# The first layer's output projection, norms and quantised FFN as one stage by query block; the pair attention's output products dealt over two steps

## The chip, the cores and the metric

The program runs on one core of a Trainium2 chip. The metric is the device time of one execution in microseconds, median of three runs. A profiled execution has a time of its own, and a span (first to last instruction) a little shorter.

## The reference

Four layers over the same residual stream of 8 sequences of 256 tokens, 128 wide (2048 tokens in all; here 16 tiles of 128 tokens, 4 query blocks of 512). Each layer is a gated cross-attention followed by a gated FFN, both on a layer norm of the stream:

```python
x = x + tanh(g_xattn[n]) * cross_attention_n(layernorm(x), ctx)
x = x + tanh(g_ffn[n])   * ffn_n(layernorm(x))
```

The change touches layer 0, and the attention of layers 1 and 3. Layer 0's attention has 16 heads of width 8. Its result goes through an output projection of 128x128. Its FFN is fake-quantised: both activations are rounded to integers against the largest absolute value over the *whole* tensor, so that nothing of the first product can start before all 2048 normalised tokens are known, and nothing of the second before all of the hidden tensor is known.

```python
def _act_fake_quant(x, clip_factor):
    scale = sigmoid(clip_factor) * max(abs(x)) / 127
    return clip(round(x / scale), -128, 127) * scale
xq = _act_fake_quant(x, clip_x)                       # 2048 x 128
h  = silu(xq @ quant(w_gate).T) * (xq @ quant(w_up).T)   # 2048 x 352
y  = _act_fake_quant(h, clip_down) @ quant(w_down).T
```

Layers 1 and 3 have 16 heads of width 64, attended over 256 keys within a sequence, with an output projection of 1024x128.

## The kernel before, in words

The program is a chain of stages. Each stage is an `nc.Block()`: five instruction streams (TensorE "pe", ScalarE "act", VectorE "dve", GpSimd "pool", SyncE "sp") that run in the order in which they are written and wait for each other on semaphores; all engines meet at the end of a block. After most blocks `retire` clears that stage's semaphores, one instruction each, on GpSimd, before GpSimd may go on to the next block. PSUM has 8 banks of 512 columns, `ps[:, bank, :]`.

**Layer 0 between its attention and layer 1** is five blocks, each over all 2048 tokens:
1. `attention_small_heads` ends: the last heads are stored to DRAM (`o_dram`), and SyncE waits for these stores (L567).
2. `gathered_projection` (L1511): the heads come back from DRAM, tile by tile, as 128x128 (L1521, 16 DMAs on two queues), are transposed (L1533), copied (L1547), multiplied by `wo0` (L1538) and added to the stream `M.x` (L1554).
3. `layernorm` (L414): statistics (L438 to L450) in two halves of 8 tiles, `rstd` by a power on GpSimd (L468), 16 normalisations (L455), 16 transposes (L475), and four copies (L486).
4. `quantised_ffn` (L1559): the largest value along each partition (L1607), then over the partitions by GpSimd's `partition_all_reduce` (L1600); three passes over 2048 columns that scale, round and clip (L1619 to L1621); 12 jobs (query block, chunk of the 352 hidden columns), each a gate product, an up product, a SiLU on ScalarE (L1594) and a multiply on VectorE (L1626). Then the largest hidden value: three reductions of 2048 columns (L1631), a second all-reduce (L1602), nine passes of rounding (L1641 to L1644), 48 fp32 down products (L1666), and four additions to the stream (L1649).
5. `layernorm` again, for layer 1 (with hi/lo fp16 copies, L488, L461). Then `attention_pairs` begins; its engines wait for two memsets of GpSimd (L846, L847) before the first product (L909).

**`attention_pairs`** (L787, layers 1 and 3) works on *units*: a query block and a pair of heads, 32 in each layer; a unit is two *half* steps `i` (one sequence each). The order is written out by hand: in step `i` TensorE issues

```python
scores(i + 1)         # L876 x12, then waits for r_done(i + 1), then L884 x8
max_scores(i + 2)     # L897
queries_keys(i + 3)   # L909 to L914
turn(i // 2 - 1)      # even steps, L960: 4 fp32 transposes
values((i + 1) // 2)  # odd steps, L924 to L926: 12 products
project((i - 3) // 2) # odd steps, L972 to L976: 12 products
weighted(i)           # L948 to L952: 24 products; max_rows(i + 2), L931, in their middle
```

VectorE issues in the same step: `normalised(i-1)` (L1056, L1058), `largest(i+2)` (L1065, after L897), `queries_keys` (L1079, after ScalarE's L1018), `turned` (even, L1086) or `values` (odd, L1093), `add` (odd, once in 8 units, L1101) and `max_rows(i+2)` (L1073), which gives r_done(i+2). ScalarE: the exponentials (L1005, after L884), L1018, L1024 or L1030, L1012. GpSimd: two subtractions L859 for each half.

## Time and profile before

| | us |
|---|---|
| median of 3 runs | 2148.47 (2147.4 to 2151.1) |
| the profiled execution | 2147.12 |
| its span | 2145.3 |
| layer 0, last head to layer 1's first product (L770 to L909) | 106.25 |
| TensorE / VectorE / ScalarE / GpSimd busy over the span | 82% / 62% / 59% / 52% |

The page gives the busy share of each engine over the whole span and in 40 slices; with the stages so different, a window for each stage says more. TensorE's busy time is modelled: overlapping products are counted from issue to end, so that the starts of neighbouring rows show better than the busy share where it waits. "Idle before" in a row is the time that the engine stood still before it, and what ended it.

### The profile page before, as it was taken

What the parts mean: (1) busy time and instruction counts of PE and PEld (TensorE: products, weight loads), DVE (VectorE), ACT (ScalarE), POOL (GpSimd) and SP (SyncE); (2) the same over time, 40 slices, a digit from 0 to 9 for tenths busy, and PEclk for the clock granted to TensorE, in tenths of its full rate; (3) what the DMA queues carried; (4) which work ended last, traced back from release to release, by engine and by line L of the source; (5) the groups of instructions that cost most, each with busy time, mean ns of one, the idle gap of its engine ahead of it and who ended that gap; (6) DMA issues with size and microseconds to landing.
All of it is one profiled execution on the core that took longest, in us unless ns stands there. A gap on an engine that the chain in (4) does not pass through costs nothing. (4 is left out here: it accounts for less than half of the span.)

```text
span 2145.3 us, 55182 instructions
## 1 busy us (share of the span) xinstructions
PE 1769.2 (82%) x22168; PEld 1236.0 (58%) x22169; DVE 1329.7 (62%) x2556; ACT 1272.8 (59%) x1627; POOL 1109.8 (52%) x1052
## 2 busy tenths in 40 slices
PE   1699636999947769999999999999736839999778
PEld 1244325888845626666666666666535727888645
DVE  3767376888864366555555555555244547888765
ACT  3357423777734326777777777777624527777553
POOL 2100003555542337777777777777752336775534
PEclk9779858999968859999999999999957969999899
DMA  6401100000032010000000000000122111000000
GB/s 175 80 6 11 27 0 2 3 3 3 2 102 74 25 47 11 11 14 11 10 13 12 11 10 14 11 10 11 32 83 56 36 48 34 3 3 3 2 6 16
DMA packets 95263, 55.20 MB, mean 26 GB/s; under 512 B 43341, under 2 KB 88728, under 8 KB 94918
## 3 DMA queue, kind: packets, MB, share of 16 engines
q1 hardware_dynamic: 86820, 42.61, 8.2%
q0 software_dynamic: 3584, 6.36, 0.9%
q8 instruction: 181, 2.97, 0.6%
q10 hardware_dynamic: 4610, 2.71, 0.5%
q14 instruction: 68, 0.56, 0.1%
HBM read 30.16 MB, written 13.75 MB: 20 GB/s over the span
## 5 line engine op out<-in xcount | busy, mean ns | idle before, releaser
L1422 POOL TENSOR_TENSOR aw_p_lo<-aw_p,aw_p_hi 128x512 f16<-128x512 f32 x512 | 576.5, 1158 | 191.0 <-issue 168.8
L1438 DVE TENSOR_REDUCE aw_max_part<-ps 128x1 f32<-128x512 f32 x512 | 351.2, 690 | 289.7 <-PE ps L1244 284.9
L859 POOL TENSOR_TENSOR ap_p_lo<-ap_p,ap_p_hi 128x512 f16<-128x512 f32 x256 | 291.0, 1158 | 181.6 <-issue 173.9
L1374 ACT ACTIVATE aw_p<-ps 128x1024 f32<-128x1024 f32 x256 | 260.0, 1015 | 206.1 <-PE ps L1275 204.0
L1289 PE MATMUL ps<-ctx_hi_lo,aw_p_hi 128*128 128x97 f16 x2048 | 288.9, 206 | 2.5 <-POOL aw_p_lo L1422 2.5
L1291 PE MATMUL ps<-ctx_hi_lo,aw_p_hi 128*128 128x96 f16 x2048 | 288.0, 207 | 0.0
L1293 PE MATMUL ps<-ctx_hi_lo,aw_p_lo 128*128 128x97 f16 x2048 | 287.4, 204 | 0.0
L1381 ACT ACTIVATE aw_p_hi<-aw_p 128x1024 f16<-128x1024 f32 x256 | 270.6, 1057 | 8.1
L1291 PEld LDWEIGHTS ps<-ctx_hi_lo,aw_p_hi 128*128 128x128 f16 x2048 | 197.9, 97 | 25.2
L1289 PEld LDWEIGHTS ps<-ctx_hi_lo,aw_p_hi 128*128 128x128 f16 x2048 | 196.5, 96 | 12.1 <-POOL aw_p_lo L1422 4.7
L1293 PEld LDWEIGHTS ps<-ctx_hi_lo,aw_p_lo 128*128 128x128 f16 x2048 | 201.9, 99 | 0.0
L1244 PE MATMUL ps<-ctxT_hi,aw_queries 96*128 96x512 f16 x512 | 197.4, 390 | 4.6 <-DVE aw_max_part L1438 4.5
L1265 PE MATMUL ps<-aw_queries,aw_keys 128*128 128x512 f16 x512 | 195.7, 382 | 0.8 <-ACT aw_p L1374 0.7
L1266 PE MATMUL ps<-aw_queries,aw_keys 128*128 128x512 f16 x512 | 195.3, 381 | 0.0
L1005 ACT ACTIVATE ap_p<-ps 128x1024 f32<-128x1024 f32 x128 | 131.1, 1024 | 95.0 <-PE ps L884 95.0
L1065 DVE TENSOR_REDUCE ap_neg_max<-ps 128x4 f16<-128x1024 f32 x128 | 156.8, 1225 | 45.6 <-PE ps L897 45.6
L468 POOL TENSOR_TENSOR ln_rstd<-ln_var_eps,neg_half 128x8 f32<-128x8 f32 x10 | 16.5, 1658 | 302.7 <-DVE ln_var_eps L450 238.5
L2178 POOL DMA_INDIRECT result_scratch<-sf_y,sf_token_at x64 | 63.7, 995 | 158.9 <-ACT sf_y L2368 144.2
L1012 ACT ACTIVATE ap_p_hi<-ap_p 128x1024 f16<-128x1024 f32 x128 | 134.8, 1053 | 0.0
L948 PE MATMUL ps<-ap_v_hi,ap_p_hi 128*128 128x65 f16 x1024 | 113.3, 194 | 4.6 <-POOL ap_p_lo L859 4.3
L950 PE MATMUL ps<-ap_v_lo,ap_p_hi 128*128 128x64 f16 x1024 | 113.2, 192 | 0.0
L952 PE MATMUL ps<-ap_v_hi,ap_p_lo 128*128 128x65 f16 x1024 | 112.6, 193 | 0.0
(464 smaller groups left out, 4979.8 us busy)
## 6 DMA issues: line engine op xcount, KB each, us to landing
sf_weights_raw<-in_L_w SPq DMA_DIRECT2D x24, 256.0 KB, 4.2
slot_scratch<-at_empty_rows SPq DMA_DIRECT2D x16, 260.0 KB
sf_fetched<-slot_scratch SPq DMA_DIRECT2D x16, 260.0 KB, 2.9
sf_weights_raw<-in_L_w SPq DMA_DIRECT2D x8, 512.0 KB, 3.9
x_norm<-result_scratch SPq DMA_DIRECT2D x8, 256.0 KB, 4.0
aw_queries<-aw_queries SPq DMA_DIRECT2D x32, 64.0 KB, 1.9
aw_queries<-aw_q_lo SPq DMA_DIRECT2D x32, 64.0 KB, 2.0
raw<-in_L_q SPq DMA_DIRECT2D x3, 512.0 KB, 11.9
```

Source lines behind the costliest of these rows:

```text
L859: nc.gpsimd.tensor_tensor(p_lo[:, i % 2, h, :], p[:, i % 2, h, :], p_hi[:, i % 2, h, :], ALU.subtract).then_inc(lo_done, 1)
L1065: nc.vector.tensor_reduce(NM[:, i % 2, :].rearrange("p (h r) -> p h r", h=2)[:, :, 0:2], ps[:, MB:MB + 2, :].rearrange("p h (t k) -> p h t ...
L1244: nc.tensor.matmul(ps[:, max_bank(b, k), :], S1[0:DC, b % 4, t * P:(t + 1) * P], M.ct_hi[0:DC, kb * QB:(kb + 1) * QB], start=True, stop=Tr ...
L1265: nc.tensor.matmul(o, K1[:, ks], S1[:, c, :], start=True, stop=False)
L1266: nc.tensor.matmul(o, K2[:, ks], S2[:, c, :], start=False, stop=False)
L1289: nc.tensor.matmul(o, p_hi[:, n % 4, cols], M.cv[:, kt, 0:DA], start=kt + t == 0, stop=False, skip_group_check=True)
L1291: nc.tensor.matmul(o[:, 0:DC], p_hi[:, n % 4, cols], M.cv[:, kt, VW:VW + DC], start=False, stop=False, skip_group_check=True)
L1293: ins = nc.tensor.matmul(o, p_lo[:, n % 4, cols], M.cv[:, kt, 0:DA], start=False, stop=kt == NT - 1, skip_group_check=True)
L1374: nc.scalar.activation(p[:, n % 2, :].rearrange("p (b q) -> p b q", b=2), s, ACT.Exp, scale=1.0 / QS).then_inc(exp_done, 1)
L1381: nc.scalar.activation(p_hi[:, n % 4, :], p[:, n % 2, :], ACT.Copy).then_inc(hi_done, 1)
L1422: nc.gpsimd.tensor_tensor(p_lo[:, n % 4, cols], p[:, n % 2, cols], p_hi[:, n % 4, cols], ALU.subtract).then_inc(lo_done, 1)
L1438: nc.vector.tensor_reduce(mpart[:, b % 2, k:k + 1], ps[:, max_bank(b, k), :], AX.X, ALU.max).then_inc(m_done, 1)
```

## The change

`gathered_projection`, `quantised_ffn`, and the two `layernorm` calls around them (layer 0's second and layer 1's first) are replaced by one block, `first_ffn`, that works by query block q (4 tiles):

- The gather of blocks 0 to 2 is issued by SyncE inside the attention (before block 2 of the next query block's heads); the last one right after the stores, two DMAs on each of two queues.
- Projection, addition, statistics, power (of 128x4 instead of 128x8) and normalisation run by block; the largest values are taken from `M.xn`, before the transposes.
- The maximum over the partitions is no longer an all-reduce on GpSimd. VectorE makes a diagonal matrix of the column, TensorE multiplies it by ones (fp32), and VectorE reduces the PSUM row.
- The rounding has two passes (min, then max and + ROUND) of 512 columns; the subtraction of ROUND, with the conversion to bf16 or fp16, goes to ScalarE (VectorE for the first block).
- The hidden maxima are taken job by job, between the multiplies.
- The down product takes fp16 integers and a down weight split into two fp16 halves: 96 fp16 products instead of 48 fp32 ones. The weights' split is made in `prepare`, by six instructions instead of three.
- The addition, layer 1's statistics, norm, transposes and hi/lo copies follow in the same block.
- `retire` has 36 semaphores to clear behind the new block.

In `attention_pairs` the 12 products of `project` are dealt: 6 in the odd step, as before, and 6 in the next even step. `add` goes to the even step, and the loop runs one step longer.

```diff
@@ build
-            layernorm(nc, M, 2 * n, split=True, plain=False)
+            if n != 1:
+                layernorm(nc, M, 2 * n, split=True, plain=False)
             if n == 0:
-                attention_small_heads(nc, M)
-                gathered_projection(nc, M)
+                gathered = [nc.alloc_semaphore(f"gathered{q}") for q in range(NQ)]
+                attention_small_heads(nc, M, gathered)
+                first_ffn(nc, M, gathered)
+                continue
...
-            layernorm(nc, M, 2 * n + 1, split=False, plain=True)
-            quantised_ffn(nc, M)
@@ prepare
-                    nc.vector.tensor_copy(M.wdT[0:IC[c], c, :], M.ps[0:IC[c], 2, c * P:(c + 1) * P])
+                    o = M.ps[0:IC[c], 2, c * P:(c + 1) * P]
+                    link(nc.vector.tensor_scalar(M.wd_hi[0:IC[c], c, :], o, WDS, None, ALU.mult))
+                    nc.vector.scalar_tensor_tensor(M.wd_lo[0:IC[c], c, :], o, WDS, M.wd_hi[0:IC[c], c, :],
+                                                   ALU.mult, ALU.subtract)
@@ attention_small_heads, sync
+                def gather(q):
+                    for i in range(2):
+                        sp.wait_ge(o_stored[i], 2 * (q + 1) * 4 * 16)
+                    for t in range(q * TQ, (q + 1) * TQ):
+                        gather_tile(sp, t)
                 for b in range(NB):
                     qb, g = block_of(b)
+                    if g == 2 and qb:
+                        gather(qb - 1)
@@ attention_pairs
-        steps = range(-3, NH + 2)
+        steps = range(-3, NH + 3)
...
-                    for t in range(TQ):
+                    for t in (2 * half, 2 * half + 1):
...
-                    if i % 2 and is_unit((i - 3) // 2):
-                        project((i - 3) // 2)
+                    if is_unit((i - 3) // 2):
+                        project((i - 3) // 2, 1 - i % 2)
...
-                    if i % 2 and is_unit((i - 3) // 2) and (i - 3) // 2 % NP == NP - 1:
-                        add((i - 3) // 2 // NP)
+                    if i % 2 == 0 and is_unit(i // 2 - 2) and (i // 2 - 2) % NP == NP - 1:
+                        add((i // 2 - 2) // NP)
@@ first_ffn, tensor
+                for q in range(NQ - 1):
+                    turn_heads(q)
+                for q in range(NQ - 1):
+                    project(q)
+                turn_heads(NQ - 1)
+                project(NQ - 1)
+                for q in range(NQ):
+                    turn(q, 0, q, n_turned)
...
+                nc.tensor.matmul(ps[:, 4, 0:P], ones[:], diag[:, 0, :], start=True, stop=True).then_inc(mx_ready, 1)
...
+                            nc.tensor.matmul(o, hq[0:w, c, at:at + P], M.wd_hi[0:w, c, :], start=c == 0, stop=False)
+                            ins = nc.tensor.matmul(o, hq[0:w, c, at:at + P], M.wd_lo[0:w, c, :], start=False,
+                                                   stop=c == 2)
@@ first_ffn, scalar
+                for q in range(NQ):
+                    if q < NQ - 1:
+                        act.wait_ge(tmp_done, 2 * (q + 1) + 2)
+                        nc.scalar.activation(xq[:, tokens(q + 1)], tmp[:, tokens(q + 1)], ACT.Identity,
+                                             bias=unround[:]).then_inc(xq_done, 1)
+                    for c in range(3):
+                        gates(3 * q + c)
@@ first_ffn, vector
+                add_heads(0)
+                statistics(0, 0)
+                add_heads(1)
+                statistics(1, 0)
+                normalise(0, 0)
+                add_heads(2)
+                statistics(2, 0)
+                normalise(1, 0)
+                largest(0)
+                normalise(2, 0)
+                largest(1)
+                largest(2)
+                add_heads(3)
+                statistics(3, 0)
+                normalise(3, 0)
+                largest(3)
...
+                    V.scalar_tensor_tensor(h[0:w, c, tokens(q)], ps[0:w, 4 + k % 4, :], us[0:w, c:c + 1],
+                                           gated[0:w, k % 2, :], ALU.mult, ALU.mult).then_inc(h_done, 1)
+                    if k:
+                        largest_h(k - 1)
...
+                def rounded(q):
+                    both = ((h[:, 0:2, tokens(q)], invh[:, 0:1]), (h[0:IC[2], 2, tokens(q)], invh[0:IC[2], 0:1]))
+                    for v, s in both:
+                        V.tensor_scalar(v, v, s, QMAX, ALU.mult, ALU.min).then_inc(hr_done, 1)
+                    for i, (v, s) in enumerate(both):
+                        dve.wait_ge(hr_done, 4 * q + 1 + i)
+                        V.tensor_scalar(v, v, -QMAX - 1.0, ROUND, ALU.max, ALU.add).then_inc(hr_done, 1)
...
+                rounded(0)
+                rounded(1)
+                rounded(2)
+                add(0)
+                statistics(0, 1)
+                rounded(3)
+                normalise(0, 1)
+                add(1)
+                statistics(1, 1)
+                add(2)
+                statistics(2, 1)
+                normalise(1, 1)
+                add(3)
+                statistics(3, 1)
+                normalise(2, 1)
+                inputs(0)
+                normalise(3, 1)
+                inputs(1)
+                inputs(2)
+                inputs(3)
```

## Rows read from the trace of the kernel before

**Rows 1.** Busy time in windows, from the last head to layer 1's first product.

```profile
243.27:277.41 34.14, 13.34 (x64) 10.55 (x64) 14.23 (x54) 6.26 (x10) 3.32 (x2) 0.65 0.15 34
277.41:285.94 8.53, 0.00 (x0) 0.00 (x1) 4.58 (x10) 0.00 (x0) 0.38 (x1) 0.53 0.00 0
285.94:304.87 18.93, 8.07 (x23) 3.10 (x24) 16.10 (x19) 8.23 (x12) 0.38 (x1) 0.68 0.00 0
304.87:347.97 43.10, 18.19 (x112) 16.60 (x112) 25.46 (x63) 2.39 (x4) 3.31 (x2) 0.64 0.00 1
347.97:349.52 1.55, 0.00 (x0) 0.00 (x1) 0.00 (x0) 0.00 (x0) 1.29 (x3) 1.00 0.00 0
```

**Rows 2.** Timeline: start us, us, engine line op; the gather, transposes and projection.

```profile
247.56 6.11 SPq L1521 DMA_DIRECT2D x_norm<-o_scratch  x8
...
251.88 1.12 PE L1533 MATMUL ps<-ident,x_norm 128*128 128x128 f32 x4 [9.23 <-DMA x_norm<-o_scratch]
...
258.65 4.77 PE L1538 MATMUL ps<-wo,x_normT 128*128 128x128 f32 x32
...
260.61 0.75 DVE L1554 SCALAR_TENSOR_TENSOR x_res<-ps,gates,x_res 128x512 f32<-128x512 f32 x1 [17.33 <-PE ps L1538]
...
264.51 1.64 DVE L438 BATCH_NORM_STATS2 ln_stats<-x_res 128x6 f32<-128x128 f32 x8 [0.30 <-PEq L1516]
...
269.47 4.18 DVE L455 TENSOR_SCALAR x_norm<-x_res,ln_mean,ln_rstd 128x128 f32<-128x128 f32 x16
```

**Rows 3.** Groups of GpSimd instructions by line: busy and mean ns, then idle before.

```profile
L1786 POOL TENSOR_TENSOR de_rstd<-de_var_eps,neg_half 128x4 f32<-128x4 f32 x4 | 4.2, 1046 | 4.1 <-DVE de_var_eps L1955 4.1
```

**Rows 4.** Timeline, quantised FFN, and at 58 us a tensor_scalar of 352 columns.

```profile
58.45 0.33 DVE L384 TENSOR_SCALAR w_down_rounded<-w_down_rounded 128x352 f32<-128x352 f32 x1
...
275.31 1.28 ACT L1594 ACT_TABLE_LOAD   x1
...
280.94 0.38 POOL L1600 PARTITION_ALL_REDUCE qf_max_all<-qf_max  x1 [9.63 <-issue]
...
283.40 1.23 DVE L1620 TENSOR_SCALAR qf_tmp<-qf_tmp 128x2048 f32<-128x2048 f32 x1
...
287.31 9.70 DVE L1626 SCALAR_TENSOR_TENSOR qf_hidden<-ps,qf_up_scale,qf_gated 128x512 f32<-128x512 f32 x12 [1.42 <-ACT qf_gated L1594]
...
297.04 6.67 DVE L1631 TENSOR_REDUCE qf_hmax<-qf_hidden 128x1 f32<-128x2048 f32 x3
```

**Rows 5.** Timeline behind a retire; VectorE's row gives the block's end.

```profile
608.62 1.65 DVE L2401 BATCH_NORM_STATS2 sf_stats<-x_res 128x6 f32<-128x128 f32 x8 [0.32 <-PEq L838]
...
610.29 0.33 POOL L2154 MEMSET sf_index_back<- 128x1 f32 x8 [7.62 <-issue]
```

**Rows 6.** Window of the pair attention, 15 units (columns as in rows 1).

```profile
420.00:535.20 115.20, 111.59 (x2065) 95.08 (x2064) 99.07 (x182) 91.47 (x121) 68.23 (x60) 1.00 0.01 3
```

**Rows 7.** Timeline of one unit's TensorE, then of its VectorE.

```profile
451.49 0.39 PE L884 MATMUL ps<-ap_max_rows,pick 64*128 64x128 f16 x8
...
453.49 0.22 PE L931 MATMUL ps<-ident,ap_neg_max 128*128 128x128 f16 x1
...
454.56 0.27 PE L876 MATMUL ps<-ap_qk_hi,ap_qk_lo 64*128 64x256 f16 x2
455.07 0.40 PE L884 MATMUL ps<-ap_max_rows,pick 64*128 64x128 f16 x8 [0.23 <-DVE ap_max_rows L1073]
...
456.95 0.22 PE L972 MATMUL ps<-wo_hi,ap_o_turned_hi 128*128 128x128 f16 x1
...
457.63 0.19 PE L948 MATMUL ps<-ap_v_hi,ap_p_hi 128*128 128x65 f16 x1
...
454.73 0.28 DVE L1073 CAST ap_max_rows<-ps 128x128 f16<-128x128 f32 x1
...
458.39 0.28 DVE L1073 CAST ap_max_rows<-ps 128x128 f16<-128x128 f32 x1
```

**Rows 8.** Who waited for whom, 380 to 590 us: total us, times, longest.

```profile
PEld ps L884 <- DVE ap_max_rows L1073: 14.8, 30, 0.5
```

More of the change, by code:

```diff
@@ L743, in _ @@
                                              bias=M.b0q[:, g:g + 1]).then_inc(h_done, 1)
+                for i in range(2):
+                    act.wait_ge(o_stored[i], NB // 2 * 4 * 16)
+                for t in range(NT - TQ + 1, NT, 2):
+                    gather_tile(act, t)
             @block.vector
@@ L962, in turn, with project @@
                     ins.then_inc(t_ready, 1)
[L964 removed]
+                def project(u, half):
                     qb, pair = block_of(u)
@@ L1588, in _, with gates @@
                 nc.scalar.activation(sig[:], M.clip[:], ACT.Exp, scale=-1.0).then_inc(exp_done, 1)
-                for k, (q, c) in enumerate(jobs):
+                for q in range(NQ):
+                    act.wait_ge(o_turned, q + 1)
+                    nc.scalar.activation(M.xt[:, tokens(q)], ps[:, q, :], ACT.Copy).then_inc(o_done, 1)
+                for q in range(NQ):
+                    act.wait_ge(n_turned, q + 1)
+                    act.wait_ge(y1_ready, q + 1)
+                    nc.scalar.activation(M.xt[:, tokens(q)], ps[:, q, :], ACT.Copy).then_inc(xt_done, 1)
+                act.wait_ge(set_up, 3)
+                def gates(k):
+                    q, c = JOBS[k]
                     w = IC[c]
@@ new lines, in inputs @@
+                def inputs(q):
+                    act.wait_ge(x_turned, q + 1)
+                    nc.scalar.activation(M.xt_hi[:, tokens(q)], ps[:, 4 + q, :], ACT.Copy).then_inc(xhi_done, 1)
+                for q in range(NQ):
+                    act.wait_ge(hr_done, 4 * q + 4)
+                    nc.scalar.activation(hq[:, 0:2, tokens(q)], h[:, 0:2, tokens(q)], ACT.Identity, bias=unround[:]
+                                         ).then_inc(hq_done, 1)
+                    nc.scalar.activation(hq[0:IC[2], 2, tokens(q)], h[0:IC[2], 2, tokens(q)], ACT.Identity,
+                                         bias=unround[0:IC[2], :]).then_inc(hq_done, 1)
@@ L1597, in _ @@
+                for q in range(NQ):
+                    inputs(q)
             @block.gpsimd
             def _(pool):
-                pool.wait_ge(xmax, 1)
-                nc.gpsimd.partition_all_reduce(mall[:], mx[:], P, RMAX).then_inc(xmax_all, 1)
-                pool.wait_ge(hmax, 1)
-                nc.gpsimd.partition_all_reduce(hall[:], hm[:], P, RMAX).then_inc(hmax_all, 1)
+                nc.gpsimd.memset(ones[:], 1.0).then_inc(set_up, 1)
+                nc.gpsimd.memset(hm[:], 0.0).then_inc(set_up, 1)
@@ new lines, in normalise, with add_heads @@
+                def normalise(q, k):
+                    dve.wait_ge(rstd_done, k * NQ + q + 1)
+                    for t in range(q * TQ, (q + 1) * TQ):
+                        V.tensor_scalar(M.xn[:, t, 0:D], M.x[:, t, :], mean[:, k, t:t + 1], rstd[:, k, t:t + 1],
+                                        ALU.subtract, ALU.mult).then_inc(normed, 1)
+                def add_heads(q):
+                    dve.wait_ge(y1_ready, q + 1)
+                    x = M.x[:, tiles(q), :].rearrange("p t f -> p (t f)")
+                    V.scalar_tensor_tensor(x, ps[:, 4 + q, :], M.gate[:, 0:1], x, ALU.mult, ALU.add).then_inc(x1_done, 1)
+                    dve.wait_ge(x1_done, q + 1)
@@ new lines, in _ @@
+                link(V.reciprocal(inv[:], sx[:]))
+                dve.wait_ge(xt_done, NQ)
+                for q in range(NQ):
+                    V.tensor_scalar(tmp[:, tokens(q)], M.xt[:, tokens(q)], inv[:, 0:1], QMAX, ALU.mult, ALU.min
+                                    ).then_inc(tmp_done, 1)
+                    dve.wait_ge(tmp_done, 2 * q + 1)
+                    V.tensor_scalar(tmp[:, tokens(q)], tmp[:, tokens(q)], -QMAX - 1.0, ROUND, ALU.max, ALU.add
+                                    ).then_inc(tmp_done, 1)
+                    if q == 0:
+                        dve.wait_ge(tmp_done, 2)
+                        V.tensor_scalar(xq[:, tokens(0)], tmp[:, tokens(0)], ROUND, None, ALU.subtract
+                                        ).then_inc(xq_done, 1)
@@ L1623, in _, with largest_h @@
+                dve.wait_ge(set_up, 3)
+                def largest_h(k):
+                    q, c = JOBS[k]
+                    w = IC[c]
+                    dve.wait_ge(h_done, k + 1)
+                    V.tensor_reduce(hm[0:w, k:k + 1], h[0:w, c, tokens(q)], AX.X, ALU.max, apply_absolute_value=True
+                                    ).then_inc(hm_seen, 1)
+                for k, (q, c) in enumerate(JOBS):
                     w = IC[c]
@@ new lines, in add, with inputs @@
+                def add(q):
+                    dve.wait_ge(y_ready, q + 1)
+                    x = M.x[:, tiles(q), :].rearrange("p t f -> p (t f)")
+                    V.scalar_tensor_tensor(x, ps[:, q, :], sh[:, 1:2], x, ALU.mult, ALU.add).then_inc(x_done, 1)
+                    dve.wait_ge(x_done, q + 1)
+                def inputs(q):
+                    dve.wait_ge(xhi_done, q + 1)
+                    V.tensor_tensor(M.xt_lo[:, tokens(q)], ps[:, 4 + q, :], M.xt_hi[:, tokens(q)], ALU.subtract)
```

266 lines of the change are left out of this document (148 added, 118 removed).

## The prediction

> **What bounds the kernel now.** I read four views. First the windows between layer 0's last head and layer 1's first product [rows 1]: 106.25 us in five stretches, in which VectorE is busy for 60.4 and TensorE's clock is mostly 0.5 to 0.7 of full. No engine is full; the blocks stand one behind the other, each over all 2048 tokens, and the idle time is between them. The reader should see two long stretches: 34.14 us up to the largest input value and 43.10 us from the rounding of the hidden values to layer 1's inputs. Second, the timeline of that stretch [rows 2, 4], for the price of each operation. Third, GpSimd behind the ends of blocks [rows 5]. Fourth, the pair attention. There TensorE looks full, 111.59 of 115.20 us busy [rows 6], but its busy time is modelled, and the starts of its products tell more. In a unit of 115.20/15 = 7.68 us the last score products of one step start at 454.56 and the next ones (L884), which would follow 0.11 later, only at 455.07, when VectorE's copy of the maxima (454.73 + 0.28) has come [rows 7]. So TensorE stands still 0.40 us in each unit; the waits show 30 such stalls in 210 us [rows 8], about one for each 7.68 us.
>
> **The stage of layer 0, part by part.** All against the profiled execution's time.
>
> *Up to the largest input value* (before: 34.14 [rows 1]). The last gather still has to wait for the last stores; it is issued at about 247.0 instead of 247.56, since it is ahead of the block's end. The block's end then waits for the two DMAs that each queue issues, 6.11/8 = 0.76 each [rows 2], so TensorE starts at about 248.9 on heads that are there already. Three groups of transposes (1.12 each) and the first group of products (4.77/4 = 1.2) bring VectorE's first addition to 253.6; the last gather lands meanwhile, some 2.8 us behind its last issue as before, so the DMA's wait is covered. From there VectorE sets the pace: per block an addition 0.75, statistics 1.64/2 = 0.82 and their small operations 0.84 (the two halves take 264.51 to 269.47, less 3.28, shared by two), normalisation 4.18/4 = 1.05 [rows 2], and the largest values, 6.67/3 = 2.22 for 2048 columns, thus 0.62 with its fixed part [rows 4]: 4.1 per block, 16.3 in all. Only the last block has nothing to cover the power, 1.05 for four columns [rows 3] and 0.25 on the way. That ends at 271.2: 27.9, a gain of 6.2.
>
> *To the first integers* (8.53 before [rows 1]; 3.5 of it are GpSimd, which begins its all-reduce at 280.94 though its input was there at 277.41 [rows 1, 4]). Now: a reduction and a diagonal 0.45, the product 0.5 (no row has it by itself; between 0.3 and 1.0), a reduction of 128 columns 0.3, the scales 0.6, and three passes of 512 columns. A pass costs 0.33 for 352 columns and 1.23 for 2048 [rows 4], a slope of 0.53 us per thousand, so 0.42 for 512 and with a scale operand and the wait 0.45: 3.2. Gain 5.3.
>
> *The hidden values* (18.93 before). ScalarE makes block 1's integers before it may start on the gates: two passes on VectorE 0.9, its own 0.65, then the table load of 1.28, which lay under the wait for the maximum before [rows 4] and now lies on the path, then a SiLU: 3.6 until the first multiply, where it was 1.4. The multiplies cost 9.70/12 = 0.81 [rows 4] and each maximum 0.62, so 12 x 1.43 = 17.2, which nothing covers, as VectorE is the bound. The maximum over partitions and the scales take 1.9. Together 22.7, a loss of 3.8. ("ScalarE: Activation LUTs", section "What ACT_TABLE_LOAD costs", of the Trainium skill gives 1.28 us for the load and 1.38 more for a drain, 2.66 in all; the row agrees on the load, 1.28, and shows no drain. By that rule this stretch would be 24.1 and the whole 1.4 us slower.)
>
> *From the rounding to layer 1's inputs* (43.10 before). Rounding: four blocks of four passes, 0.66, 0.40, 0.60, 0.35, by the slope above: 2.05 each, 8.2 in all. If the view of two rows of 512 columns does not run at the rate of the 2048 columns, the passes of 1024 take twice as long, 4.3 more; I take the faster, as the row that is nearest, and keep the other for the range. ScalarE's two copies (1.7) and TensorE's 24 fp16 products, (457.63 - 456.95)/12 = 0.057 each at full clock [rows 7], twice that at half, 2.7, bring the first addition 0.7 behind VectorE's arrival. Then 4 x 4.1 = 16.3 for addition, statistics, normalisation and the low halves (0.62), and 0.9 at the end for the last transpose and copy. The down product of the other blocks (13.9 us alone before) lies under this. 26.1: a gain of 17.0.
>
> *To the first product* (1.55 before). Layer 1 waits for two memsets of GpSimd (1.29), which now stand behind 36 clears of semaphores. Rows 5: with 24 semaphores to clear, GpSimd begins at 610.29 where VectorE began at 608.62, 0.07 each. So 2.5 for the clears: 4.2, a loss of 2.6. The queue past which this moves is GpSimd's, and TensorE, ScalarE and VectorE all wait for it.
>
> Sum: 6.2 + 5.3 - 3.8 + 17.0 - 2.6 = 22.1. The split of the down weights adds three short, chained instructions ahead of the first norm, 0.3 each by the row of 0.33 [rows 4], bounds 0.5 and 1.5: -0.9. Net 21.2. The 12 gathers that SyncE issues inside the attention take 3 us each four; a block of heads lasts about 8, and its stores are double-buffered, so I cost them at nothing. Without that cover it would be at most 3 x 3 us.
>
> **The pairs.** Each step is as long as the slower of two paths from one L884 to the next. VectorE's path (L884, L897, largest, low halves, copy, L884) takes 455.07 - 451.49 = 3.58 in the step with the turned heads, where TensorE waited, and 458.67 + 0.06 - 455.07 = 3.66 in the other. TensorE's own work is 3.18 (3.58 less the 0.40) and, as the unit lasts 7.68, 4.10. Six products are 0.34 [rows 7]. Moved, TensorE's work is 3.52 and 3.76, and the steps last 3.58 and 3.76: 7.34, a gain of 0.34 a unit, or 0.33 for caution. Of 32 units in a layer I count 29.5; the rest is ramp. The addition `add` now stands in the step where VectorE sets the time: about 0.66 each where 0.22 showed, three times a layer, -1.3. Two layers: 2 x (9.7 - 1.3) = 16.8. Between the bounds of nothing and 0.43 a unit (all of the stall), 0 to 25.
>
> 2147.12 - 21.2 - 16.8 = 2109.1 for the profiled execution; the median of the runs is 1.35 above the profiled one, so 2110.5.
>
> **Rivals.**
> *A: the pairs give nothing* (0.15). For it: TensorE is 97% busy [rows 6], and the products of a step might end no sooner however they are dealt. Against it: a stall of 0.40 in each unit that the starts of the products show. 2147.12 - 21.2 + 1.35 = 2127.3. ("Perfetto Trace Analysis", section "Identifying the Most-Contended Engine", of the Trainium skill says that matmul busy time is no good measure and to take the weight loads' share; here that is 95.08/115.20 = 83%. By that rule TensorE has room and A is less likely.)
> *B: the stage gives less* (0.12): the streams are written out in order, and a ScalarE or TensorE that waits for one block's semaphore holds back the next; with the slow two-row passes (4.3), a longer product (0.5 twice) and the table, the stage saves 15. 2147.12 - 15 - 16.8 + 1.35 = 2116.7.
> *C: slower* (0.02). The six products moved to the even step stand ahead of `weighted`, in whose middle L931 gives the maxima that VectorE copies. L931 comes 2.0 after L884 now [rows 7] and would come 2.33 after it; VectorE gets to it 3.24 after it. From 0.9 us of delay on it decides, and each unit would grow by what exceeds it. To eat the stage's 21.2 it would have to add 0.36 a unit over today's 7.68. Then 2150 and above. The slack of 0.9 against a shift of 0.34 speaks against it.
> *My forecast* has 0.69, another 0.02 for no change of any kind.
>
> **The range.** Likeliest case by itself: the stage 18 to 26, the pairs 12 to 21: 2101 to 2119. With A inside, 2102 to 2129. A change under 0.2% (4.3 us) is about what the measurement can't tell: faster 0.96, same 0.02, slower 0.02.
>
> **What the profile would show.** The last head to layer 1's first product: 84 us instead of 106; no partition all-reduce; VectorE over 80% busy from the first addition on; a table load between the first integers and the first SiLU; GpSimd's memsets 3 us behind the block's end. In the pairs: a unit of 7.34 us, steps of 3.58 and 3.76, and the L884 stall under 0.1. Wrong it would be if units stay at 7.68, or if VectorE shows gaps above 1 us inside the stage.

## The result, and the profile after

The changed kernel takes 2117.68 us (median of 4 runs, 2106.59 to 2124.28), the kernel before 2149.78 beside it (its three runs and a fourth): a ratio of 0.9842, 95% interval 0.9804 to 0.9881. Forecast were 2110.5 us and a range of 2102 to 2129. In two later series of 5 runs each it took 2108.77 (ratio 0.9826, 0.9802 to 0.985) and 2111.18 (0.9848, 0.9829 to 0.9867). The profiled execution below took 2106.59 us, span 2104.7.

First the windows of the stage after, from the last head (237.91) on; its five stretches answer to [rows 1].

```profile
core 0: us, PE busy (x) PEld busy (x) DVE busy (x) ACT busy (x) POOL busy (x), PEclk, DMA share, GB/s
237.91:266.12 28.21, 12.33 (x64) 9.74 (x64) 16.38 (x71) 4.55 (x9) 4.40 (x7) 0.67 0.08 13
266.12:270.10 3.98, 0.77 (x2) 0.50 (x2) 2.68 (x11) 0.43 (x1) 0.00 (x0) 0.50 0.00 0
270.10:291.20 21.10, 10.97 (x25) 3.02 (x26) 18.74 (x37) 11.19 (x16) 0.00 (x0) 0.58 0.00 1
291.20:316.58 25.38, 12.28 (x112) 9.80 (x112) 24.11 (x84) 9.32 (x12) 5.05 (x4) 0.70 0.00 1
316.58:320.68 4.10, 0.00 (x0) 0.00 (x1) 0.01 (x1) 0.00 (x0) 1.28 (x3) 0.50 0.00 0
```

Together 82.77 us, where it was 106.25. VectorE does 61.9 us of work here, as it did 60.4 before: what went is its idle time, from 45.9 to 20.9 us. In the fourth stretch it is busy 24.11 of 25.38 us.

Then the timeline of the same stage, the lines that answer to [rows 2, 4] and carry the terms of the sum.

```profile
248.36 0.75 DVE L1742 SCALAR_TENSOR_TENSOR x_res<-ps,gates,x_res 128x512 f32<-128x512 f32 x1 [3.49 <-PE ps L1598]
264.27 1.12 DVE L1736 TENSOR_SCALAR x_norm<-x_res,ff_mean,ff_rstd 128x128 f32<-128x128 f32 x4 [1.12 <-POOL ff_rstd L1703]
265.43 0.69 DVE L1747 TENSOR_REDUCE ff_x_max<-x_norm 128x4 f32<-128x512 f32 x1
267.59 0.29 DVE L1773 TENSOR_REDUCE ff_x_max_all<-ps 128x1 f32<-128x128 f32 x1 [0.95 <-PE ps L1618]
271.78 1.28 ACT L1671 ACT_TABLE_LOAD   x1
273.08 1.27 ACT L1671 ACTIVATE ff_gated<-ps,ff_gate_scale 128x512 f32<-128x512 f32 x2
273.85 1.41 DVE L1803 SCALAR_TENSOR_TENSOR ff_h<-ps,ff_up_scale,ff_gated 128x512 f32<-128x512 f32 x2 [1.19 <-PE ps L1629]
...
282.02 0.74 DVE L1803 SCALAR_TENSOR_TENSOR ff_h<-ps,ff_up_scale,ff_gated 128x512 f32<-128x512 f32 x1
282.68 0.67 DVE L1796 TENSOR_REDUCE ff_h_max<-ff_h 128x1 f32<-128x512 f32 x1
283.27 0.74 DVE L1803 SCALAR_TENSOR_TENSOR ff_h<-ps,ff_up_scale,ff_gated 96x512 f32<-96x512 f32 x1
...
290.36 0.29 DVE L1812 TENSOR_REDUCE ff_h_max_all<-ps 128x1 f32<-128x128 f32 x1 [0.89 <-PE ps L1632]
...
291.20 1.15 DVE L1820 TENSOR_SCALAR ff_h<-ff_h,ff_inv_h 128x1024 f32<-128x1024 f32 x2
297.91 0.75 DVE L1828 SCALAR_TENSOR_TENSOR x_res<-ps,ff_scale_h,x_res 128x512 f32<-128x512 f32 x1 [0.64 <-PE ps L1641]
314.61 1.97 DVE L1833 TENSOR_TENSOR x_normT_lo<-ps,x_normT_hi 128x512 f16<-128x512 f32 x3
319.40 0.31 POOL L872 MEMSET ap_neg_max<- 128x256 f16 x1 [6.23 <-issue]
320.68 0.39 PE L935 MATMUL ps<-x_normT_hi,wq_hi 128*128 128x256 f16 x1 [5.46 <-POOL ap_v_hi L873]
```

The brackets are the reading: from the first addition to the last low half VectorE stands still five times, 1.12 for the last power, 0.95 and 0.89 for the two products with ones, 1.19 for the first multiply, 0.64 for the first down product, under 5 us in all (pauses under 0.2 are not counted); it is busy 90% of that time, where over 80% was forecast. Two of them lie above the 1 us that the prediction had named as a sign of being wrong. Both are in its own sum, the power with 1.05 and 0.25 and the first multiply in the 3.6 us until it starts, so the sign was set too low. One job of multiply and maximum lasts 1.25 (282.02 to 283.27).

In the pairs one unit is 7.34 us. TensorE's timeline (L910 is the L884 of before), the window of one unit, and the waits between 360 and 550 us, against [rows 6 to 8]:

```profile
431.19 0.27 PE L902 MATMUL ps<-ap_qk_hi,ap_qk_lo 64*128 64x256 f16 x2
431.36 0.40 PE L910 MATMUL ps<-ap_max_rows,pick 64*128 64x128 f16 x8
...
433.25 0.22 PE L998 MATMUL ps<-wo_hi,ap_o_turned_hi 128*128 128x128 f16 x1
...
435.12 0.39 PE L910 MATMUL ps<-ap_max_rows,pick 64*128 64x128 f16 x8
```

```profile
431.36:438.70 7.34, 7.34 (x140) 6.37 (x139) 6.53 (x13) 6.12 (x8) 4.56 (x5) 1.00 0.01 3
```

```profile
PEld ps L910 <- DVE ap_max_rows L1100: 6.2, 24, 0.8
```

The step that ends at 435.12 is 3.76 long and the next 3.58, to 438.70. The waits of the weight loads were 0.49 each (14.8 in 30) and are 0.26 (6.2 in 24, one per unit). By the products' own starts little of that is left: the row maxima start at 431.36 where 431.30 (431.19 + 0.11) would follow without a wait.

Three steps of each layer are longer, the ones in which VectorE has `add` in front of the copy of the maxima:

```profile
397.78 0.39 PE L910 MATMUL ps<-ap_max_rows,pick 64*128 64x128 f16 x8
402.01 0.40 PE L910 MATMUL ps<-ap_max_rows,pick 64*128 64x128 f16 x8 [0.56 <-DVE ap_max_rows L1100]
```

Such a step lasts 4.24 (4.23 in these two rows) where its like lasts 3.58, 0.66 more; in the kernel before it was 4.32 against 4.10, 0.22 more.

Landmarks from all the traces give the time of each part of the program, and show what the change touches and what varies by itself. Each number is the difference of two starts in a timeline (layer 0's first exponential; its last head; layer 1's first product; GpSimd's memset behind layer 1's attention; the power of the next layer norm; GpSimd's memset that opens layer 3's attention; its first memset behind it; the end):

| us | before | after | after_again | after_third | stage_only | deal_only |
|---|---|---|---|---|---|---|
| start to layer 0's attention | 115.49 | 116.21 | 115.90 | 117.93 | 116.14 | 116.87 |
| layer 0's attention | 127.49 | 121.41 | 126.68 | 126.87 | 126.85 | 121.29 |
| the stage | 106.54 | 83.06 | 83.22 | 83.57 | 83.41 | 106.20 |
| layer 1's attention | 260.77 | 252.48 | 252.29 | 252.48 | 262.18 | 252.65 |
| its sparse FFN | 148.48 | 153.81 | 149.45 | 149.52 | 149.58 | 149.64 |
| layer 2 and its FFN | 1008.88 | 1008.03 | 1009.14 | 1008.60 | 1008.55 | 1009.17 |
| layer 3's attention | 262.26 | 253.89 | 254.12 | 254.31 | 263.29 | 253.88 |
| to the end | 115.39 | 115.81 | 116.10 | 116.62 | 113.50 | 116.31 |

(The last head is counted from the start of its instruction here, 0.29 earlier than in the windows.)

### The profile page after: what moved, and what is told of

Its sections match the earlier page's. It is cut to its first block and busy times, and to the rows that moved or that the text cites. A ratio compares the mean times of both kernels' runs of the same rounds, so it can differ in the third digit from the quotient of the medians.

```text
span 2104.7 us, 55264 instructions
## 1 busy us (share of the span) xinstructions
PE 1751.7 (83%) x22172; PEld 1223.8 (58%) x22173; DVE 1330.5 (63%) x2616; ACT 1281.0 (61%) x1638; POOL 1112.6 (53%) x1057
## 5 line engine op out<-in xcount | busy, mean ns | idle before, releaser
L1106 DVE TENSOR_TENSOR ap_qk_lo<-ps,ap_qk_hi 128x512 f16<-128x512 f32 x128 | 88.5, 692 | 33.0 <-ACT ap_qk_hi L1045 33.0
```

## Experiments: the two edits apart

These ran beside the kernel before at 2145.38 us.

**The changed kernel once more.** No edit.

> The changed kernel once more, since its four runs lay between 2106.6 and 2124.3 us where those of the kernel before lay within 5.4. Theory: the stage and the pairs give 23.5 and 16.7 us whatever the run, and the rest of the spread lies in stages that the change does not touch, through TensorE's granted clock (0.906 in the fastest run, 0.895 in the slowest). Then in this profile the last head to layer 1's first product is 82 to 84 us again and a unit of the pairs 7.34, and any difference from the first profile lies in layer 0's attention or behind layer 1's attention. Rival: the new code varies itself; then the stage or the units differ by more than 2 us.

2108.77 us (2105.32 to 2113.08), ratio 0.9826 (0.9802 to 0.985). The table has its trace: stage and pairs repeat within 0.2 us each. The first profile had won a further 5.3 in layer 0's attention and lost 4.4 in the sparse FFN.

**The stage alone.** The changed kernel with the pairs' products as before:

```diff
-                    for t in (2 * half, 2 * half + 1):
+                    for t in range(TQ):
...
-                    if is_unit((i - 3) // 2):
-                        project((i - 3) // 2, 1 - i % 2)
+                    if i % 2 and is_unit((i - 3) // 2):
+                        project((i - 3) // 2)
```

> The changed kernel with the 12 output products of a unit back in the odd step. Theory (the two edits are independent): 16.7 us slower than the changed kernel, so about 2133, units of 7.68 us, and the stage as in the changed kernel, 83 us. Rival A (TensorE is full, the dealing gives nothing and the whole gain is the stage's): within 3 us of the changed kernel, 2118.

2127.28 us, ratio 0.9913 (0.9892 to 0.9934). The stage is 83.41, the attention layers 262.2 and 263.3, 1.4 and 1.0 over those of before. Of layer 1's 1.4, 1.3 lies in the first step behind its first row maxima, and that step varies with the granted clock in it, whatever the edit: 3.66 us at 1.00 in after_again, 3.82 at 0.95 in after_third, 4.64 at 0.77 in late_clears, 5.28 at 0.67 here. The steps of a unit, in its timeline:

```profile
433.20 0.40 PE L910 MATMUL ps<-ap_max_rows,pick 64*128 64x128 f16 x8 [0.23 <-DVE ap_max_rows L1099]
437.30 0.39 PE L910 MATMUL ps<-ap_max_rows,pick 64*128 64x128 f16 x8
440.87 0.40 PE L910 MATMUL ps<-ap_max_rows,pick 64*128 64x128 f16 x8 [0.23 <-DVE ap_max_rows L1099]
```

4.10 with all 12 products, then 3.57 ended by VectorE: 7.67, the unit of before, with the stall of [rows 7].

**The dealing alone.** The kernel before, with the same lines edited the other way.

> The kernel before with only the output products dealt, 6 and 6. Theory: 16.7 us faster than before, about 2133, units of 7.34 us, layer 0's stage 106 us as before. Rival A: no change, 2149.8, units of 7.68.

2133.69 us, ratio 0.994 (0.9919 to 0.996). The stage stays at 106.20, the attention layers are 252.65 and 253.88, 8.1 and 8.4 less. Each edit gives its part without the other: rival A has fallen, and so has B. The medians are coarser than the traces: the stage alone is 18.1 us under the kernel before and the dealing alone 11.7 (16.7 expected), 29.8 together, where both at once gave 36.6. Each of the three has a 95% interval of 4 to 5 us to either side.

**All 12 products in the even step.**

```diff
-                    for t in (2 * half, 2 * half + 1):
+                    for t in (range(TQ) if half else ()):
```

> The changed kernel with all 12 products of a unit in the even step and none in the odd one. Theory (each step lasts as long as the slower of VectorE's path, 3.58 and 3.66 us, and TensorE's work): TensorE has 3.18 + 0.68 = 3.86 in the even step and 4.10 - 0.68 = 3.42 in the odd one, so 3.86 + 3.66 = 7.52 us a unit, 0.18 above the changed kernel, 10.6 us over 59 units: about 2117 to 2129 for a single run. Rival (what counts is how unevenly TensorE's work lies): 0 and 12 is like 12 and 0, 7.68.

2117.6 us in one run; the attention layers 256.40 and 258.45, 4.1 and 4.3 above the run beside it. The steps:

```profile
430.89 0.39 PE L910 MATMUL ps<-ap_max_rows,pick 64*128 64x128 f16 x8
434.54 0.40 PE L910 MATMUL ps<-ap_max_rows,pick 64*128 64x128 f16 x8
...
438.40 0.39 PE L910 MATMUL ps<-ap_max_rows,pick 64*128 64x128 f16 x8
```

3.65 and 3.86, 7.51 in sum. By the prediction's paths the odd step is VectorE's 3.66 (TensorE has 4.10 - 0.68 = 3.42) and the even one TensorE's 3.18 + 0.68 = 3.86. Both steps agree within 0.01. The two layers lose 8.4 us together and not the 10.6 expected: in the steps with `add`, 4.24 in the changed kernel, this edit costs nothing, as VectorE's path is the longer one there in both.

## Experiments: inside the stage

Of each of these there is one run, beside the kernel before at 2147.49. As layer 0's attention takes one of two values by itself, the stage's own duration is compared, against the 83.22 of after_again.

**The table load early.** A SiLU of two columns on a spare tile, behind ScalarE's last copy of layer 0's norm:

```diff
                 act.wait_ge(set_up, 3)
+                nc.scalar.activation(spare[:], M.clip[:], ACT.Silu)
```

> The changed kernel with one small SiLU (128x2, its result unused) on ScalarE before the integers, so that the table load of 1.28 us falls where ScalarE waits for the largest input value. Theory: the load was on the path, and VectorE's first multiply comes about 1.2 us earlier; the stage from the last head to layer 1's first product goes from 83.1 to 82.0. Rival: the first multiply waits for the products or for VectorE's own passes, 83.1 as before.

The stage is 82.23, 1.0 less. ScalarE's timeline:

```profile
272.24 0.60 ACT L1662 ACTIVATE x_normT<-ps 128x512 f32<-128x512 f32 x1 [5.28 <-PE ps L1605]
272.86 1.28 ACT L1664 ACT_TABLE_LOAD   x1
274.15 0.20 ACT L1664 ACTIVATE ff_spare<-clips 128x2 f32<-128x2 f32 x1
277.27 0.72 ACT L1678 ACTIVATE ff_x_int<-ff_x_rounded,ff_unround 128x512 bf16<-128x512 f32 x1 [2.92 <-DVE ff_x_rounded L1785]
277.90 1.25 ACT L1672 ACTIVATE ff_gated<-ps,ff_gate_scale 128x512 f32<-128x512 f32 x2
```

The load lies under the wait for the maximum, and the first SiLU follows the integers at once. In the changed kernel the load ends at 273.06 and the SiLU starts at 273.08, so the load cost its own 1.28 at the most and nothing behind it. ("ScalarE: Activation LUTs", section "What ACT_TABLE_LOAD costs", of the Trainium skill adds a drain of 1.38 us; of the 2.66 that it gives, moving the load would have returned more than the 1.0 measured.)

**The clears late.** The stage's 36 semaphores are cleared behind layer 1's attention.

```diff
-                first_ffn(nc, M, gathered)
+                first_sems = first_ffn(nc, M, gathered)
...
                 attention_pairs(nc, M, n)
+                retire(nc, first_sems)
```

> The changed kernel with the 36 semaphores of the stage cleared behind layer 1's attention instead of ahead of it. Theory: 36 x 0.07 = 2.5 us less, stage 80.6; layer 1's attention unchanged, and the clears then add 2.5 behind it, ahead of GpSimd's first work of the sparse FFN, where they are partly under the statistics. Rival: GpSimd's memsets wait for the end of the block and not for the clears: 83.1.

The stage is 80.76, 2.5 less: that price was right. But layer 1's attention, to the memset behind it, is 255.66, 3.4 more. Of these 1.0 is its first step (4.64 against 3.66, the clock again); the other 2.4 are the clears, which stand on the path there as well. Nothing is gained.

**All gathers behind the last stores.** SyncE and ScalarE issue the 16 together, as in the kernel before, but ahead of the block's end.

```diff
-                    if g == 2 and qb:
-                        gather(qb - 1)
...
-                for t in range(NT - TQ, NT, 2):
+                for t in range(0, NT, 2):
                     gather_tile(sp, t)
```

> The changed kernel with all 16 gathers behind the last stores, 8 on each of two queues. Theory: the block's end waits for six more issues on each queue, 6 x 0.76 = 4.6 us, and all of the stage shifts by it: 87.7. Rival 1: the gathers inside the attention cost as much there as they save; then layer 0's attention gets shorter by some of it (127 or 121 us now, by the clock). Rival 2: hidden, 83.1.

The stage is 87.29, 4.1 more: TensorE's first transposes start at 250.80, 10.9 us behind the last head (239.95), where it was 6.4. Layer 0's attention took 121.33 here, as in the first profile with the gathers inside it (121.41), so the 12 gathers cost nothing there.

**The maxima by GpSimd's all-reduce.** Both products with ones go; GpSimd does what it did before.

```diff
-                V.tensor_scalar(diag[:, 0, :], M.ident[:], mx1[:, 0:1], None, ALU.mult).then_inc(dx_ready, 1)
...
+                pool.wait_ge(dx_ready, 1)
+                nc.gpsimd.partition_all_reduce(mall[:], mx1[:], P, RMAX).then_inc(mx_ready, 1)
+                pool.wait_ge(dh_ready, 1)
+                nc.gpsimd.partition_all_reduce(hall[:], hm1[:], P, RMAX).then_inc(mh_ready, 1)
```

> The changed kernel with both maxima over the partitions taken by GpSimd's all-reduce as before the change. Theory (switching GpSimd between this instruction and the power costs a load of code): the first costs 3.5 + 0.6 instead of 1.7, +2.4; the second 0.5 instead of 1.5, -1.0; then layer 1's first power comes some 6 us behind its variance as before the change, where VectorE has 2 us of other work: +4. The stage goes from 83.1 to 88 to 89. Rival (the diagonal with the product costs what the all-reduce does): 83.1 +- 1.

Only 1.6 more (84.79), where I had expected about 5: two of my three terms held. GpSimd's timeline:

```profile
269.88 1.01 POOL L1697 TENSOR_TENSOR ff_rstd<-ff_var_eps,neg_half 128x4 f32<-128x4 f32 x1 [5.25 <-DVE ff_var_eps L1728]
276.54 0.38 POOL L1703 PARTITION_ALL_REDUCE ff_x_max_all<-ff_x_max_row  x1 [5.66 <-issue]
298.17 0.35 POOL L1705 PARTITION_ALL_REDUCE ff_h_max_all<-ff_h_max_row  x1 [21.25 <-DVE ff_h_max_row L1804]
308.42 1.94 POOL L1697 TENSOR_TENSOR ff_rstd<-ff_var_eps,neg_half 128x4 f32<-128x4 f32 x1 [9.90 <-DVE ff_var_eps L1728]
```

The first all-reduce costs 2.3 more than diagonal, product and reduction (2.4 expected): VectorE waits 3.99 for it where it waited 0.95. It starts 5.65 behind the end of the power, though its input, of 272.8, had been there for 3.6. The second follows its input at once and is 1.0 cheaper than diagonal, product and reduction. The third cost that I expected, a late power on the way back, does not show: at 308.42 it is ended by VectorE's variance.

So the price is neither the instruction (0.38) nor a fixed time behind its input. From where it counts, the kernel before helps to tell:

```profile
275.12 2.29 DVE L1607 TENSOR_REDUCE qf_max<-x_normT 128x1 f32<-128x2048 f32 x1 [1.47 <-PEq L432]
...
339.67 3.31 POOL L468 TENSOR_TENSOR ln_rstd<-ln_var_eps,neg_half 128x8 f32<-128x8 f32 x2 [35.48 <-issue]
```

There the all-reduce starts 9.63 behind the last power [rows 4], but 5.8 behind 275.12, the start of its block, before which GpSimd can't come to it. Both traces fit some 5.7 us from the moment at which GpSimd comes to the all-reduce, paid only as far as the input comes sooner. The way back was late there, and VectorE waited 5.22 for it: the power starts at 339.67, 8.6 behind the start of its block (331.1) and 6.0 behind its variance. With all in one block GpSimd comes to the power right behind the all-reduce, 9.9 us ahead of the variance, and whatever it needs is over by then. That the 5.7 are due to the change of kind is not shown: the second all-reduce had 21.25 us until its input came, in which they would have been hidden in any case. What GpSimd does in that time no row names.

**The down products in fp32.** One fp32 weight in place of the two halves, fp32 integers, 48 products in place of 96.

```diff
-                            nc.tensor.matmul(o, hq[0:w, c, at:at + P], M.wd_hi[0:w, c, :], start=c == 0, stop=False)
-                            ins = nc.tensor.matmul(o, hq[0:w, c, at:at + P], M.wd_lo[0:w, c, :], start=False,
+                            ins = nc.tensor.matmul(o, hq[0:w, c, at:at + P], M.wd32[0:w, c, :], start=c == 0,
```

> The changed kernel with the fp16 pairs of down products undone: one fp32 weight and fp32 integers, 48 fp32 products where it has 96 of fp16. The values of the weight are then a single fp32 and not a pair of fp16. My theory (the gain behind the rounding comes from the order by block, under VectorE's 2.0 us per block of rounding, and not from the product's type): a block's 12 fp32 products take about 3.5 us at half clock where 24 of fp16 take 2.65, the first addition is 0.8 late and the four blocks run at 3.5 and not 2.65 at worst, so the stage is at most 3.5 us longer (83.1 to 86.6), and 1.5 longer if the clock is up; the set-up is 0.9 shorter because no low half is made. The rival (the fp16 products are the gain): the stage is over 5 us longer.

It ran later, beside after_third. The stage is 85.92 against 83.57: 2.35 more. The first block's products, in its timeline, with the addition that waits for them:

```profile
301.94 8.24 PE L1638 MATMUL ps<-w_downT,ff_h_int 128*128 128x128 f32 x52 [4.81 <-ACT ff_h_int L1687]
...
307.09 0.75 DVE L1825 SCALAR_TENSOR_TENSOR x_res<-ps,ff_scale_h,x_res 128x512 f32<-128x512 f32 x1 [3.01 <-PE ps L1638]
```

A block takes 5.1 us (301.94 to about 307.06), not the 3.5 that I expected. VectorE's wait grows from 0.64 to 3.01, by 2.37, and this is the whole difference: the other three blocks' products are under VectorE's work in either type. Of the 17.7 us that the fourth stretch won, the type gives 2.35. The rest is what the order by block in one stage gives, by subtraction. VectorE's waits name most of it: before, it waited 5.58, 2.27, 1.93 and 1.93 for down products, 11.7 in all, where 0.64 is left, and 5.22 for the power above, where nothing is left. The set-up is 1.0 shorter, as expected: the first statistics start 0.97 behind the first of the weight's copies (62.17 to 63.14), where it is 1.95 in after_third (62.16 to 64.11).

## Experiments: the last refinements

These ran with down_fp32, and the kernel before at 2143.29.

**The changed kernel, third.**

> The changed kernel itself, beside the others of this call. Expected from its two profiles: the stage at 83.1 us, layer 1's and layer 3's attention at 252.4 and 254.0, layer 0's attention at either 121.4 or 126.7 (the one part that differed by over 5 us between its profiles), and the sparse FFN 1 between 149 and 154; a median of 2107 to 2119. If the difference in layer 0's attention is a draw of the clock it takes one of the two values here again, not one between; if it is the position of a buffer or of code it is the value of one and the same kernel each time.

2111.18 us (2108.27 to 2112.93), ratio 0.9848 (0.9829 to 0.9867). Layer 0's attention: 126.87, one of the two values.

**3 products in the odd step, 9 in the even one.**

```diff
-                    for t in (2 * half, 2 * half + 1):
+                    for t in ((1, 2, 3) if half else (0,)):
```

> The changed kernel with 3 of a pair's 12 output products at the odd step and 9 at the even one, where it has 6 and 6. My theory (a step takes the longer of TensorE's and ScalarE's work in it): odd step max(3.58, 3.42), even step max(3.77, 3.76) as the products move 0.18 from the one to the other, so 7.35 per unit and layer 1's and layer 3's attention within 1 us of the changed kernel's 252.4 and 254.1. The rival (the products cost in proportion to how unevenly they stand, halfway between 6 and 6 and 0 and 12): 0.07 per unit more, 2 us more in each of the two layers.

```profile
432.85 0.40 PE L910 MATMUL ps<-ap_max_rows,pick 64*128 64x128 f16 x8
436.54 0.39 PE L910 MATMUL ps<-ap_max_rows,pick 64*128 64x128 f16 x8
440.19 0.40 PE L910 MATMUL ps<-ap_max_rows,pick 64*128 64x128 f16 x8
```

The attention layers are 252.29 and 253.94, those of the changed kernel, and the unit is 7.34. The single steps in my expectation were put down wrongly, and only the sum holds: by the prediction's paths the even step is TensorE's 3.18 + 0.51 = 3.69 and the odd one VectorE's 3.66, and the timeline has 3.69 and 3.65. Between 6 and 6 and 3 and 9 the sum of the two maxima is flat.

**The best.** The table load early, VectorE's `add` behind `max_rows` in its step, and the clears in GpSimd's own order within layer 1's attention, behind its bias addition (7 us of waiting follow there):

```diff
+                retire(nc, done)
...
-                    if i % 2 == 0 and is_unit(i // 2 - 2) and (i // 2 - 2) % NP == NP - 1:
-                        add((i // 2 - 2) // NP)
                     if is_half(i + 2):
                         max_rows(i + 2)
+                    if i % 2 == 0 and is_unit(i // 2 - 2) and (i // 2 - 2) % NP == NP - 1:
+                        add((i // 2 - 2) // NP)
```

> The changed kernel with three edits more: ScalarE's table load ahead of the first SiLU's wait (an extra activation on a spare tile), the clears of the first stage's semaphores in GpSimd's order inside layer 1's attention, behind its bias addition, and VectorE's addition of a head's products behind the next unit's row maxima instead of ahead of them. My theory: the first stage (last head to layer 1's first product) falls by 0.9 (the load, as the run with the load early) and 2.4 (the clears, as the run with the clears late) from 83.1 to about 79.8 us; the clears stand where GpSimd waits for VectorE in any case, so nothing is given back and layer 1's attention stays at 252.4 or less. The addition's move takes up to 1.3 us per head-pair layer off TensorE's wait for the row maxima: 0 to 1.3 per layer. In sum 3.3 to 5.9 us under the changed kernel run beside it, about 2104. The rival: the clears cost layer 1's attention what they free, wherever they stand (as 3.3 us where they were put in the way before), and the addition's move makes the sum of the heads late: stage 79.8, attention 255.5, and the total within 2 us of the changed kernel's.

2101.37 us (2094.51 to 2106.39), ratio to before 0.9801 (0.9776 to 0.9826), where after_third has 0.9848; no run of the one overlaps a run of the other. GpSimd's and PE's lines:

```profile
316.65 1.04 POOL L1705 TENSOR_TENSOR ff_rstd<-ff_var_eps,neg_half 128x4 f32<-128x4 f32 x1 [2.44 <-DVE ff_var_eps L1732]
321.38 0.31 POOL L872 MEMSET ap_neg_max<- 128x256 f16 x1 [3.68 <-POOLq L1586]
...
334.14 2.28 POOL L886 TENSOR_TENSOR ap_p_lo<-ap_p,ap_p_hi 128x512 f16<-128x512 f32 x2 [7.08 <-ACT ap_p_hi L1040]
```

```profile
PEld ps L911 <- DVE ap_max_rows L1101: 4.2, 24, 0.2
```

The stage is 79.55 (4.0 less than beside it), layer 1's attention 251.96 (0.5 less), layer 3's 252.74 (1.6 less): 6.1 of the 9.8 between the medians. The three steps of 4.24 are gone from each layer, three times 0.66, more than the 1.3 expected; in layer 1 the first step takes 1.5 of it back (5.29 at a clock of 0.67, 3.82 at 0.95 beside it). The clears are not given back this time, since the subtraction behind them waits for ScalarE anyway. TensorE's longest wait for the maxima falls from 0.8 to 0.2. The rest of the difference between the two profiles is in parts with no edit: 1.5 before layer 0's attention and 3.1 behind layer 3's.

## Why the prediction was right

**The stage.** Predicted 84.1, measured 82.8, by stretches 27.9, 3.2, 22.7, 26.1, 4.2 against 28.2, 4.0, 21.1, 25.4, 4.1.
- *To the largest input value.* TensorE starts 6.4 behind the last head (5.6 predicted), VectorE's first addition comes at 10.45 (10.3), its 4.1 per block and the uncovered power (1.12) held. The run with late gathers shows what having three blocks' heads in place is worth: 4.1.
- *To the first integers.* The product with ones was mis-sized: 0.5 was taken out of 0.3 to 1.0, the wait is 0.95. I had read the all-reduce's 3.5 as its price; it is what was left of some 5.7 us from GpSimd's arrival when the input came. Since that is how it stood before, the reading did no harm to this term (5.3 predicted, 4.55 won), but it is no price to carry elsewhere.
- *The hidden values.* The wait for the first multiply, 3.6, is 3.75. A job was mis-sized: 1.43 was the sum of two durations, 0.81 and 0.62. Side by side they are 0.74 and 0.67 long and start 1.25 apart, as each one's start overlaps the other's end. 12 times 0.18 is 2.2, and the products and scales took 0.35 more: the term was -3.8 and came to -2.2.
- *From the rounding on.* 2.0 per block (2.05), first addition 0.64 late (0.7): the view of two rows runs at the faster rate, and the slow bound of 4.3 is out. The gain was 17.7 (17.0), of it 2.35 from the products' type. The sum got there by counting what is left, and never named the 5.22 that VectorE lost before to the late power.
- *To the first product.* 4.1 (4.2), 2.5 of it clears; taking them away gave 2.5 back.
- *The weights' split.* The first statistics behind it start at 64.21 where they started at 63.24: 0.97 for 0.9.

**The pairs.** Steps of 3.58 and 3.76 were forecast, and 431.36 to 438.70 is 7.34; the median of the steps in either layer is 3.58 and 3.76 in all three traces. Per layer 8.4 was forecast; the three traces of the changed kernel have 8.3, 8.5, 8.3 and 8.4, 8.1, 8.0. That each step is the longer of two paths is shown by four deals (12 and 0, 6 and 6, 3 and 9, 0 and 12: 7.67, 7.34, 7.34, 7.51), each of them worked out from one unit of the trace of before (3 and 9 put right only after its run). The cost of `add` (0.66 each where it was 0.22, three times a layer, 1.3) is what the steps show: 4.24 against 3.58, where it was 4.32 against 4.10. On rival A, "Perfetto Trace Analysis" of the Trainium skill, section "Identifying the Most-Contended Engine", says that matmul busy time is no good measure. The traces agree: there was room behind 97% of it, and the weight loads' share rose from 83% to 87% (6.37 of 7.34). Rival C, a delay through L931, left no sign at a shift of 0.34, nor with all 12 products in the even step. Missed was a detail: the stall was to be under 0.1, and the weight loads still wait 0.26 a unit, with 0.06 of it left between the products.

**The sum.** The stage and the two attention layers gave 40.1, 39.9 and 39.2 us in the three traces, less 0.97 for the split 39.2, 39.0 and 38.2, where 38.0 were forecast. The medians show 32.1, 36.6 and 32.1. In the third series two things make up the difference: the other parts were 2.8 longer in that profile than in the one of before, the split not counted (1.5 at the start, -0.6 in layer 0's attention, 1.0 in the sparse FFN, -0.3 and 1.2 behind them), and the median of the kernel before was 3.8 under its own profile (2147.12). Whether the 2.8 is chance or follows from the change can't be told from one trace of the kernel before; it stays open. The first median, 2117.68, lies 7.2 over the forecast, and its 4 runs are 18 us apart, where the 5 of each later series lie within 8 and 5; what the other three did is in no trace. The forecast of the median was within its range, then, but the medians won 1.4 to 5.9 us less than the 38.0 of the sum, and only the third of these gaps is followed part by part.

## What to carry to other kernels

Where every stage waits for a maximum or a power over all tokens, cut the work around that barrier into blocks, and count only what the slowest engine does in each block; the other engines' work, even products of twice the length, then costs its first block alone. Where two engines alternate, a step lasts as long as the longer of two paths: write down both paths for each step, and move work until the sum of the maxima is flat. Clears and table loads have a price that depends on their place: put them where their own engine waits anyway, and check that the queue behind them waits too.

## What the runs showed of the hardware

- GpSimd's all-reduce of 0.38 us starts 5.65 us behind a power in one trace and 5.8 behind the start of its block in the kernel before, where GpSimd comes to it each time; its input had been there for 3.5 to 3.6 us in both. A second one whose input came 21.25 us later followed it at once.
- Two neighbouring VectorE instructions of 0.74 and 0.67 start 1.25 apart, not 1.41.
- fp32 products of 128x128 took 5.1/12 = 0.43 us each at a granted clock of 0.55 (301.94 to 307.06); fp16 ones stand 0.107 apart at 0.50 (295.13 to 297.90 in the changed kernel), so a pair takes half of that.
- The first step of layer 1's attention lasted 3.66 us at a granted clock of 1.00 in it and 5.28 at 0.67, with 3.82 at 0.95 and 4.64 at 0.77 between them (after_again, stage_only, after_third, late_clears; none has an edit in it).
- Layer 0's attention took 121.3 to 121.4 us or 126.7 to 127.5, in the same code. In the 34 us that begin with its first exponential the granted clock was 0.93 in the first profile of the changed kernel, 0.74 in its second and 0.72 in the one of before; afterwards all run at 0.97 to 1.00:

```profile
116.21:150.21 34.00, 33.29 (x330) 15.73 (x329) 24.60 (x42) 24.45 (x31) 0.00 (x0) 0.93 0.10 7
```

```profile
115.90:149.90 34.00, 33.51 (x279) 14.75 (x278) 20.28 (x34) 20.47 (x27) 0.00 (x0) 0.74 0.07 5
```

```profile
115.49:149.49 34.00, 33.52 (x273) 14.68 (x275) 19.73 (x34) 19.88 (x26) 0.00 (x0) 0.72 0.07 5
```

The dealing alone, with layer 0 as in the kernel before, drew the short value as well, and the changed kernel's third profile the long one: it isn't the change. What decides when the clock rises was not tried. It is worth 5 us, more than several of the edits here, and a comparison of two single profiles would have put it down to the gathers.
